# Splitting each half of a paired matmul step into a step of its own, with new places for score and maximum units, in a windowed-attention layer

## The chip, the cores and the metric

The kernel runs on one core of one Trainium2 chip. The metric is the device time of one execution in microseconds, the median of several runs. TensorE (PE in the profile; its weight loads are PEld), VectorE (DVE), ScalarE (ACT) and GpSimd (POOL) each work through their own instructions in order; SyncE (SP) issues all transfers. They meet at semaphores only.

## The reference

A post-norm transformer layer over 16 rows (batch entries) of 512 tokens and 256 features, 16 heads of 16 features, windows of 128 tokens:

```python
qkv = (x @ Wqkv + bqkv).reshape(B, S, 3, H, Dh)
scores = jnp.einsum('bhnqd,bhnkd->bhnqk', qb, kwin) * scale     # each window sees itself and both neighbours
mask = (jnp.abs(kpos - qpos) <= W) & (kpos >= 0) & (kpos < S)
attn = jax.nn.softmax(jnp.where(mask, scores, -1e30), axis=-1)
out = jnp.einsum('bhnqk,bhnkd->bhnqd', attn, vwin) @ Wout + bout
x = layernorm(x + out)
h = relu(x @ Wq1.T + b1)                                        # Wq1, Wq2: weights rounded to -1, 0, 1
x = layernorm(x + h @ Wq2.T + b2)                               # 256 -> 1024 -> 256
```

## The kernel before

**One row, many stages.** The outer loop (`steps`, positions `at` = -2 to 16) handles a row per position, and several rows at once: while the attention of row `b` runs, the row before it goes through output projection, norms and feed-forward (the steps named in `POST`), and the row after it through its query, key and value projections. A position has four parts (`v` = 0 to 3), one for each quad of heads. I call one position a *turn* of the loop; most of them do the same work.

**Side steps.** `SIDE[v]` lists the steps of a part in TensorE's order: `qk` (query and key projection, two of them), `vp` (values), `nmt` (transposes the negative row maxima), `pv` (probabilities times values, 32 matmuls), `ut` and `ot` (transposes back), `op` (output projection), `ln1`, `x1` and `x1t` (norm, its result, its transpose), four `f1` and two `f2` (feed-forward), `xs`, `xr` and `ln2`. Most of TensorE's side steps write a pair of PSUM banks out of `shared` (two pairs, `N_PAIRS = 2`), and a step that takes a pair waits until its last reader is done (`pair_free`, line 479).

**Two halves.** The contraction is cut into the lower and upper 64 partitions. `in_halves` (line 522) and `transposes_in_halves` (line 544) issue matmuls in couples, one on each half of the array, into different banks. Once every matmul of the first half of the step is issued, the banks are exchanged, and TensorE waits on its own semaphore `s_half` until the first half has drained. Both halves are in one step. `passed()` between couples lets score and maximum units in.

**Score and maximum units.** A part has 12 score units S0 to S11 (`scores`, line 500: keys times queries into `st`, read by ScalarE's exponential, line 749) and 12 maximum units M0 to M11 (`max_scores`, line 516, into `mx`, read by VectorE, line 899) for a quad two parts on. Each has two banks, so unit i waits until the reader of unit i-2 is done. S and M work on opposite halves of the array. `weave` puts them in six groups S, M, S, M, preferably where halves are exchanged (`RUN = 2`).

**Order elsewhere.** VectorE follows `dve_order` with a `LAG` for each kind of step, ScalarE follows the list itself, with its share of a step before or after the step's exponentials, POOL masks the probabilities when units 5 and 11 are through (line 1059), and SP follows `TRANSFERS`.

## Time and profile before

| | before |
|---|---|
| runs | 1175.44 us median of 3 (1175.4 to 1178.41) |
| profiled execution | 1178.41 us, span 1176.7 us, mean granted TensorE clock 0.904 |
| instructions | 28808, of them PE matmuls 10628 |

An instruction's duration in the timeline contains the filling and draining of the array; matmuls on the two halves of the array and successive ones overlap, so the distance between starts says what one costs. PEclk is the granted TensorE clock as a share of 2.4 GHz: 1.00 is 2.4 GHz, 0.50 is 1.2 GHz, and a value between is a mix of the two over the stretch. An idle time in front of a group is put down to the engine whose semaphore came last.

### The profile page before, as it was taken

What the parts mean: (1) busy time and instruction counts of PE and PEld (TensorE: products, weight loads), DVE (VectorE), ACT (ScalarE), POOL (GpSimd) and SP (SyncE); (2) the same over time, 40 slices, a digit from 0 to 9 for tenths busy, and PEclk for the clock granted to TensorE, in tenths of its full rate; (3) what the DMA queues carried; (4) which work ended last, traced back from release to release, by engine and by line L of the source; (5) the groups of instructions that cost most, each with busy time, mean ns of one, the idle gap of its engine ahead of it and who ended that gap; (6) DMA issues with size and microseconds to landing.
All of it is one profiled execution on the core that took longest, in us unless ns stands there. A gap on an engine that the chain in (4) does not pass through costs nothing.

```text
span 1176.7 us, 28808 instructions
## 1 busy us (share of the span) xinstructions
PE 973.5 (83%) x10628; PEld 772.5 (66%) x10628; DVE 813.6 (69%) x2900; ACT 704.1 (60%) x1401; POOL 612.6 (52%) x951
## 2 busy tenths in 40 slices
PE   4798887988798888979798898879888797977866
PEld 2474776766676676767577676767677676666644
DVE  3785868678685867768686767768686867866222
ACT  3254765849485665848476584848567584835613
POOL 1124464655656555655655466565645465554522
PEclk8587899989999898999899899989989998997967
DMA  8654334344452543454263434445254434431000
GB/s 194 71 87 74 48 64 81 60 80 74 75 91 38 93 64 73 66 92 74 58 92 55 81 61 79 75 79 86 39 95 63 81 57 74 74 61 33 11 9 18
DMA packets 58026, 81.82 MB, mean 70 GB/s; under 512 B 8736, under 2 KB 28704, under 8 KB 57888
## 3 DMA queue, kind: packets, MB, share of 16 engines
q1 hardware_dynamic: 57888, 79.99, 40.9%
q8 instruction: 85, 1.39, 0.6%
q14 instruction: 53, 0.43, 0.2%
HBM read 20.19 MB, written 8.39 MB: 24 GB/s over the span
## 4 chain that ended last, share of the span: by engine, by line
PE 47%; ACT 22%; DVE 14%; issue 9%; POOL 4%; DMA 2%; SPq 1%; DVEq 0%; ACTq 0%; POOLq 0%
PE shared L538 24%; PE st L500 8%; PE shared L586 7%; DVE mx L899 7%; ACT probs L749 6%; ACT hidden L825 5%; PE mx L516 5%; ACT hid_hi L828 4%; ACT x L807 2%; PE shared L558 2%; ACT oT_x1T_hi L813 1%; DVE rmax L899 1%; ACT qk_hi L773 1%; POOL probs L1059 1%; PE shared L599 1%
## 5 line engine op out<-in xcount | busy, mean ns | idle before, releaser
L899 DVE CUSTOM_DVE_ANT_0 mx<-mx,band 128x384 f32<-128x384 f32 (+1 forms) x1024 | 479.0, 517 | 250.4 <-PE mx L516 245.5
L749 ACT ACTIVATE probs<-st 128x384 f32<-128x384 f32 (+1 forms) x768 | 365.3, 524 | 186.8 <-PE st L500 183.6
L516 PE MATMUL mx<-k_stack,q_stack 48*128 48x384 f32 (+1 forms) x1024 | 290.7, 371 | 22.3 <-DVE rmax L899 17.2
L1059 POOL TENSOR_SCALAR_AFFINE_SELECT probs<-probs 128x512 f32<-128x512 f32 (+1 forms) x256 | 127.8, 524 | 311.0 <-ACT probs L749 311.0
L500 PE MATMUL st<-q_stack,k_stack 50*128 50x384 f32 (+1 forms) x1024 | 266.7, 355 | 12.3 <-ACT probs L749 7.0
L500 PEld LDWEIGHTS st<-q_stack,k_stack 50*128 50x128 f32 x1024 | 183.8, 209 | 63.7 <-issue 30.7
L516 PEld LDWEIGHTS mx<-k_stack,q_stack 48*128 48x128 f32 x1024 | 186.0, 210 | 50.0 <-DVE rmax L899 39.5
L586 PE MATMUL shared<-probs,v_aug 128*32 128x384 f32 (+1 forms) x2048 | 165.1, 448 | 9.4 <-POOL probs L1063 7.2
L538 PE MATMUL shared<-w2q,hid_hi 64*128 64x256 f32 x1024 | 158.3, 306 | 2.0 <-POOL hid_lo L1104 1.7
L538 PE MATMUL shared<-w2q,hid_lo 64*128 64x256 f32 x1024 | 150.2, 295 | 0.0
L899 DVE DVE_READ_ACCUMULATOR2_ANT rmax<- 128x1 f32 x1024 | 144.2, 141 | 0.0
L538 PEld LDWEIGHTS shared<-w2q,hid_hi 64*128 64x128 f32 x1024 | 132.2, 203 | 3.6 <-ACT hid_hi L828 1.9
L538 PEld LDWEIGHTS shared<-w2q,hid_lo 64*128 64x128 f32 x1024 | 133.7, 203 | 0.0
L1104 POOL TENSOR_TENSOR hid_lo<-hidden,hid_hi 128x512 fp32r<-128x512 f32 x64 | 82.5, 1289 | 88.8 <-ACT hid_hi L828 88.8
L586 PEld LDWEIGHTS shared<-probs,v_aug 128*32 128x32 f32 x2048 | 91.2, 112 | 56.0 <-issue 19.3
L1063 POOL TENSOR_SCALAR_AFFINE_SELECT probs<-probs 128x512 f32<-128x512 f32 (+1 forms) x256 | 127.7, 524 | 0.0
L538 PE MATMUL shared<-oT_x1T_hi,w1q 64*128 64x512 f32 x512 | 115.6, 419 | 6.3 <-ACT hidden L825 2.0
L538 PE MATMUL shared<-oT_x1T_lo,w1q 64*128 64x512 f32 x512 | 111.7, 406 | 0.0
L825 ACT ACTIVATE hidden<-shared,b_cols 128x512 f32<-128x512 f32 x128 | 87.1, 680 | 15.1 <-PE shared L538 14.0
L792 ACT ACTIVATE u<-shared 128x512 f32<-128x512 f32 x64 | 37.5, 585 | 84.0 <-PE shared L586 84.0
L828 ACT ACTIVATE hid_hi<-hidden 128x512 fp32r<-128x512 f32 x128 | 80.8, 631 | 4.1
L982 DVE TENSOR_TENSOR hid_lo<-hidden,hid_hi 128x512 fp32r<-128x512 f32 x64 | 51.9, 810 | 40.2 <-ACT hid_hi L828 39.5
(99 smaller groups left out, 1883.5 us busy)
## 6 DMA issues: line engine op xcount, KB each, us to landing
q_stack<-qk_hi SPq DMA_DIRECT2D x128, 128.0 KB, 4.2
k_stack<-qk_hi SPq DMA_DIRECT2D x128, 128.0 KB, 5.0
x_raw<-in_xT SPq DMA_DIRECT2D x16, 512.0 KB, 5.8
q_stack<-qk_lo SPq DMA_DIRECT2D x64, 128.0 KB, 3.9
k_stack<-qk_lo SPq DMA_DIRECT2D x64, 128.0 KB, 5.5
y<-in_x SPq DMA_DIRECT2D x16, 512.0 KB, 6.3
out<-x SPq DMA_DIRECT2D x32, 256.0 KB, 2.2
probs<-in_w2T SPq DMA_DIRECT2D x1, 1024.0 KB, 10.2
```

The lines of the kernel that those rows point to most:

```text
L500: mm = pe.matmul(PST[i % N_SCORE][:, col:col + n], SK[rows, hd, W * m:W * m + W], SQ[rows, hd, q0:q0 + n], start=True, stop=True)
L516: mm = pe.matmul(PMX[i % N_MAX][:, col:col + n], SQ[rows, hd, W * m:W * m + W], SK[rows, hd, k0:k0 + n], start=True, stop=True)
L538: mm = pe.matmul(out[k][:, cols], lhs(rows), rhs(rows), start=(swap == 0 and n == 0), stop=(swap == 1 and n == count - 1), skip_group_chec ...
L586: mm = pe.matmul(out[0][32 * g:32 * g + 32, q0:q0 + width], VAUG[:, vq, m, g, :], PR[:, vq % 2, g // 2, lo:lo + width], start=(m == 0), st ...
L749: act.activation(PR[:, v % 2, g // 2, lo:lo + n], PST[i % N_SCORE][:, 0:n], ACT.Exp, scale=SCALE) \
L825: act.activation(H32[:, i, :], PG[:, 2 * k + i, :], ACT.Relu, bias=B1C[:, f:f + 1]) \
L828: act.activation(HID[0][:, f, :], H32[:, i, :], ACT.Identity).then_inc(s_hh, 1)
L899: mx = dve.tensor_tensor_reduce(ps, ps, band, 1.0, -3e38, ALU.add, ALU.max, RMAX[:, g, m:m + 1])
L982: dve.tensor_tensor(HID[1][:, f, :], H32[:, i, :], HID[0][:, f, :].bitcast(F32), ALU.subtract).then_inc(s_hld, 1)
L1059: pool.affine_select(out=pr_before, in_=pr_before, compare_op=ALU.is_ge, fill=0.0, base=0, pattern=[[0, n], [1, W]], channel_multiplier=-1)
L1063: last = pool.affine_select(out=pr_after, in_=pr_after, compare_op=ALU.is_ge, fill=0.0, base=0, pattern=[[0, n], [-1, W]], channel_multipl ...
L1104: pool.tensor_tensor(HID[1][:, f, :], H32[:, i, :], HID[0][:, f, :].bitcast(F32), ALU.subtract).then_inc(s_hlp, 1)
```

## The change

1. Each halved step becomes two entries of `SIDE`: `("start", ...)` issues the first half, the plain name the second, with the wait for `s_half` at its front. Other steps may stand between: `start qk 0`, `nmt`, `pv`, `ut 0`, `qk 0`; `start vp`, `start op`, `vp`, `op`. `pairs` hands out the two bank pairs as a queue through the whole loop.
2. `ut` is no longer tied to the `pv` of its part: the third part has none, the fourth has two. The `f1` steps follow one another; `vp` moves from between them to the first part. `ln2` comes at the end of the fourth part.
3. The 12 score and 12 maximum units of a part have places of their own, two tables in thousandths of the part's cost (`SCORES_AT`, `MAXIMA_AT`), so S and M units no longer come in couples.
4. Dummy matmuls (`WARM`): 12 couples a turn of 512 columns each on constant weights, in front of six steps, 384 matmuls in all.
5. ScalarE gets an order of its own (`act_order`, `ACT_LAG`), VectorE's lags go by single step, `TRANSFERS` is reordered, the loop has one more position (empty), and `scores` no longer waits for another quad's stack.
6. `REST_ON_POOL` shrinks from four `hid_lo` subtractions a turn on POOL (0, 2, 4, 6) to one (3), the others go to VectorE; one of four `x1` normalisations moves from ScalarE to VectorE.

```diff
 SIDE = [
-    ["nmt", "pv", "ut", "ot", "op", ("ln1", 0), ("ln1", 1), ("ln1", 2), ("ln1", 3)],
-    [("qk", 0), ("x1", 0), ("x1", 1), "nmt", "pv", ("x1", 2), "ut", ("x1", 3), "x1t", ("qk", 1), ("f1", 0)],
-    [("f1", 1), "vp", ("f1", 2), ("f1", 3), "nmt", "pv", "ut", ("xs", 0), ("xs", 1)],
-    [("f2", 0), ("ln2", 0), "xr", ("ln2", 1), "nmt", "pv", "ut", ("f2", 1), ("ln2", 2), ("ln2", 3)],
+    [("start", "qk", 0), "nmt", "pv", ("ut", 0), ("qk", 0), ("start", "ot"), "ot", ("start", "vp"),
+     ("start", "op"), "vp", "op", ("ln1", 0), ("ln1", 1), ("ln1", 2)],
+    [("ln1", 3), ("x1", 0), ("start", "qk", 1), ("qk", 1), ("x1", 1), ("x1", 2), "nmt", "pv", ("x1", 3),
+     ("ut", 1), ("start", "x1t"), "x1t", ("start", "f1", 0), ("f1", 0), ("start", "f1", 1), ("f1", 1),
+     ("start", "f1", 2)],
+    [("f1", 2), ("start", "f1", 3), "xr", ("f1", 3), "nmt", "pv", ("start", "f2", 0), ("f2", 0)],
+    [("start", "f2", 1), ("ut", 2), ("xs", 0), ("f2", 1), ("xs", 1), "nmt", "pv", ("ut", 3), ("ln2", 0),
+     ("ln2", 1), ("ln2", 2), ("ln2", 3)],
 ]
-REST_ON_POOL = (0, 2, 4, 6)
-X1_ON_DVE = ()
-RUN = 2
+REST_ON_POOL = (3,)
+X1_ON_DVE = (0,)
+SCORES_AT = ((57, 63, 184, 334, 424, 487, 492, 504, 606, 632, 712, 872),
...
+MAXIMA_AT = ((121, 126, 221, 289, 550, 575, 633, 708, 807, 844, 970, 995),
...
+WARM = {("ut", 0): 3, ("start", "x1t"): 1, ("ut", 1): 1, ("start", "qk", 1): 2, ("start", "f1", 3): 2,
+        ("start", "f1", 0): 3}
...
                     pe.wait_ge(s_nmin[v], 16 * b + 16)
-                    pe.wait_ge(s_nmin[v], 16 * b + 16)
-                    if v < 2 or stages(at)[2]:
-                        pe.wait_ge(s_stk[(v + 2) % 4], 96 * (b + v // 2) + 96)
...
-            def in_halves(out, terms, filled, passed, ready=None):
+            def one_half(out, terms, filled, passed, second, ready=None):
                 count = len(terms[0])
+                if second:
+                    exchange(passed)
+                for n in range(count):
+                    if n > 0 or not second:
                         passed()
...
+                    for rows, k in ((LOWER, second), (UPPER, 1 - second)):
...
+                for _ in range(WARM.get(whole_step, 0) if fresh else 0):
+                    for i, rows in enumerate((LOWER, UPPER)):
+                        pe.matmul(out[i], WQKV[0][rows, 0, 0:P], WQKV[0][rows, 1, 0:S], start=True, stop=True)
```

**Place 1: TensorE from the first part's `ut` to `op`.** Before: L599 is `ut`, L558 on `o_norm` is `ot`, L538 on `wout` is `op`, `st` and `mx` are score and maximum units.

```order
L500 MATMUL st<-q_stack,k_stack 128x384
L516 MATMUL mx<-k_stack,q_stack 128x384
L500 MATMUL st<-q_stack,k_stack 128x384
L516 MATMUL mx<-k_stack,q_stack 128x384
L599 MATMUL shared<-identity,u 128x64 x8
L558 MATMUL shared<-identity,o_norm 128x64 x8
L500 MATMUL st<-q_stack,k_stack 128x256 x2
L516 MATMUL mx<-k_stack,q_stack 128x256 x2
L500 MATMUL st<-q_stack,k_stack 128x384
L516 MATMUL mx<-k_stack,q_stack 128x384
L558 MATMUL shared<-identity,o_norm 128x64 x8
L538 MATMUL shared<-wout_hi,oT_x1T_hi 128x256 x2
```

And in the changed kernel: L671 are dummies, L697 is `ut 0`, L630 on `wqkv` is the second half of `qk 0`, L648 is `ot`, L589 are scores.

```order
L671 MATMUL shared<-wqkv_hi 128x512 x6
L697 MATMUL shared<-identity,u 128x64 x8
L589 MATMUL st<-q_stack,k_stack 128x384
L630 MATMUL shared<-xT_hi,wqkv_hi 128x512 x2
L630 MATMUL shared<-xT_hi,wqkv_lo 128x512 x2
L630 MATMUL shared<-xT_lo,wqkv_hi 128x512 x2
L589 MATMUL st<-q_stack,k_stack 128x384
L630 MATMUL shared<-xT_hi,wqkv_hi 128x512 x2
L630 MATMUL shared<-xT_hi,wqkv_lo 128x512 x2
L630 MATMUL shared<-xT_lo,wqkv_hi 128x512 x2
L648 MATMUL shared<-identity,o_norm 128x64 x6
L589 MATMUL st<-q_stack,k_stack 128x256 x2
```

The second half of `qk 0` has come between `ut` and `ot`, and the maximum units are gone from there; behind `ot` now comes `vp`, not `op`.

**Place 2: TensorE from the second part's `ut` to what follows `x1t`.** Before (L558 on `x` is `x1t`, L538 on `xT` is `qk 1`):

```order
L599 MATMUL shared<-identity,u 128x64 x8
L558 MATMUL shared<-identity,x 128x64 x8
L500 MATMUL st<-q_stack,k_stack 128x384
L516 MATMUL mx<-k_stack,q_stack 128x384
L500 MATMUL st<-q_stack,k_stack 128x256 x2
L516 MATMUL mx<-k_stack,q_stack 128x256 x2
L558 MATMUL shared<-identity,x 128x64 x8
L538 MATMUL shared<-xT_hi,wqkv_hi 128x512 x2
L538 MATMUL shared<-xT_hi,wqkv_lo 128x512 x2
L538 MATMUL shared<-xT_lo,wqkv_hi 128x512 x2
```

In the changed kernel (L605 is a maximum unit, L630 on `w1q` is `f1 0`):

```order
L671 MATMUL shared<-wqkv_hi 128x512 x2
L697 MATMUL shared<-identity,u 128x64 x8
L671 MATMUL shared<-wqkv_hi 128x512 x2
L648 MATMUL shared<-identity,x 128x64 x8
L589 MATMUL st<-q_stack,k_stack 128x384
L648 MATMUL shared<-identity,x 128x64 x8
L671 MATMUL shared<-wqkv_hi 128x512 x6
L630 MATMUL shared<-oT_x1T_hi,w1q 128x512 x2
L605 MATMUL mx<-k_stack,q_stack 128x384
L630 MATMUL shared<-oT_x1T_lo,w1q 128x512 x2
```

`qk 1` no longer stands between `x1t` and `f1 0`; three dummy couples and one score unit do.

**Place 3: TensorE at the second part's first score units.** Before, in the middle of `qk 0`:

```order
L538 MATMUL shared<-xT_lo,wqkv_hi 128x512 x2
L500 MATMUL st<-q_stack,k_stack 128x384
L516 MATMUL mx<-k_stack,q_stack 128x384
L500 MATMUL st<-q_stack,k_stack 128x384
L516 MATMUL mx<-k_stack,q_stack 128x384
L538 MATMUL shared<-xT_hi,wqkv_hi 128x512 x2
L538 MATMUL shared<-xT_hi,wqkv_lo 128x512 x2
```

In the changed kernel, at the start of `qk 1`, right behind the last matmuls of `op`:

```order
L630 MATMUL shared<-wout_lo,oT_x1T_hi 128x256 x2
L671 MATMUL shared<-wqkv_hi 128x512 x4
L589 MATMUL st<-q_stack,k_stack 128x384 x2
L589 MATMUL st<-q_stack,k_stack 128x256 x2
L630 MATMUL shared<-xT_hi,wqkv_hi 128x512 x2
L589 MATMUL st<-q_stack,k_stack 128x384 x2
L630 MATMUL shared<-xT_hi,wqkv_lo 128x512 x2
L589 MATMUL st<-q_stack,k_stack 128x256 x2
L630 MATMUL shared<-xT_lo,wqkv_hi 128x512 x2
L589 MATMUL st<-q_stack,k_stack 128x384
L630 MATMUL shared<-xT_hi,wqkv_hi 128x512 x2
```

Seven score units, which stood in four groups with maximum units before, now follow one another with three couples of `qk 1` between them.

## Rows read from the trace of the kernel before

**Rows 1.** The page: busy time by engine, and the chain that ended last.

```profile
PE 973.5 (83%) x10628; PEld 772.5 (66%) x10628; DVE 813.6 (69%) x2900; ACT 704.1 (60%) x1401; POOL 612.6 (52%) x951
...
PE 47%; ACT 22%; DVE 14%; issue 9%; POOL 4%; DMA 2%; SPq 1%; DVEq 0%; ACTq 0%; POOLq 0%
```

**Rows 2.** Chain in order of time: start, us, what; `x1t`'s evacuation, seven turns apart.

```profile
202.09 1.09 ACT oT_x1T_hi L813 x2
...
672.54 1.09 ACT oT_x1T_hi L813 x2
```

**Rows 3.** Stretches: us, PE, PEld, DVE, ACT, POOL busy (instructions), PEclk, DMA share, GB/s.

```profile
279.04:344.97 65.93, 56.16 (x668) 44.89 (x666) 49.65 (x181) 43.39 (x88) 38.45 (x60) 0.97 0.44 74
```

**Rows 4.** Waits of PE over the span: total us, times, longest.

```profile
PE shared L599 <- ACT u L792: 31.7, 46, 1.4
PE shared L538 <- DVE oT_x1T_lo L945: 27.5, 16, 1.8
PE shared L558 <- DVE o_norm L940: 19.2, 16, 1.4
PE shared L558 <- ACT x L807: 18.2, 32, 4.6
PE mx L516 <- DVE rmax L899: 17.2, 39, 0.8
PE shared L576 <- DVE neg_max L910: 16.6, 16, 1.9
...
PE shared L586 <- POOL probs L1063: 7.2, 14, 0.5
```

**Rows 5.** Stretches as in rows 3: `vp`, `f2 1`, `op`.

```profile
278.82:283.90 5.08, 4.87 (x65) 4.11 (x61) 4.70 (x13) 4.80 (x11) 2.19 (x2) 1.00 1.08 117
303.30:309.75 6.45, 5.68 (x80) 5.16 (x78) 5.49 (x26) 2.83 (x6) 5.38 (x9) 1.00 0.73 109
319.39:326.05 6.66, 6.66 (x73) 6.49 (x75) 5.11 (x20) 4.13 (x10) 1.95 (x4) 0.74 1.03 151
```

**Rows 6.** Timeline of PE: couples at two clocks, and a score unit beside a side step.

```profile
321.12 0.45 PE L538 MATMUL shared<-wout_hi,oT_x1T_lo 64*128 64x256 f32 x2
321.34 0.45 PE L538 MATMUL shared<-wout_lo,oT_x1T_hi 64*128 64x256 f32 x2
...
322.94 0.30 PE L538 MATMUL shared<-wout_hi,oT_x1T_lo 64*128 64x256 f32 x2
323.06 0.30 PE L538 MATMUL shared<-wout_lo,oT_x1T_hi 64*128 64x256 f32 x2
...
324.82 0.33 PE L500 MATMUL st<-q_stack,k_stack 50*128 50x384 f32 x1
324.88 0.28 PE L538 MATMUL shared<-wout_hi,oT_x1T_lo 64*128 64x256 f32 x1
...
328.00 0.43 PE L538 MATMUL shared<-xT_hi,wqkv_lo 64*128 64x512 f32 x2
328.23 0.43 PE L538 MATMUL shared<-xT_lo,wqkv_hi 64*128 64x512 f32 x2
```

**Rows 7.** Stretches as in rows 3, around the first part's `ut`, `ot` and `op`.

```profile
314.60:317.90 3.30, 1.64 (x30) 1.42 (x30) 2.32 (x10) 1.05 (x4) 2.76 (x6) 1.00 0.26 93
317.90:321.20 3.30, 1.81 (x16) 1.84 (x18) 2.66 (x9) 2.59 (x6) 0.00 (x0) 0.73 1.00 153
```

**Rows 8.** Groups by form: line engine operation, busy us, mean ns; of evacuations and units' readers.

```profile
L749 ACT ACTIVATE probs<-st 128x384 f32<-128x384 f32 x512 | 238.3, 489 | 115.7 <-PE st L500 112.5
...
L825 ACT ACTIVATE hidden<-shared,b_cols 128x512 f32<-128x512 f32 x128 | 87.1, 680 | 15.1 <-PE shared L538 14.0 <-POOL hid_lo L1104 0.2
...
L1104 POOL TENSOR_TENSOR hid_lo<-hidden,hid_hi 128x512 fp32r<-128x512 f32 x64 | 82.5, 1289 | 88.8 <-ACT hid_hi L828 88.8
...
L982 DVE TENSOR_TENSOR hid_lo<-hidden,hid_hi 128x512 fp32r<-128x512 f32 x64 | 51.9, 810 | 40.2 <-ACT hid_hi L828 39.5
...
L976 DVE TENSOR_TENSOR oT_x1T_lo<-shared,oT_x1T_hi 128x512 fp32r<-128x512 f32 x32 | 20.5, 682 | 5.3 <-ACT oT_x1T_hi L813 5.2
```

## The prediction made before the changed kernel ran

> **What bounds the kernel now.** I read the page's first and fourth part first. TensorE is the busiest engine and the last chain runs through it for 47%, with ACT at 22% and DVE at 14% [rows 1]: no engine is full, and a few engines take turns. The chain in order of time repeats itself: the same evacuation comes at 202.09 and, seven turns later, at 672.54 [rows 2], so a turn takes 470.45 / 7 = 67.2 us, and what is saved in a turn is paid back about 15 times (the positions 1 to 15; the first three and the last do part of the work). In one turn of 65.9 us TensorE is busy 56.2 us, DVE 49.7, ACT 43.4, POOL 38.5 [rows 3]. So the reader is to look for two things: the 9.7 us in which TensorE stands, and the part of its busy time in which it isn't issuing at its rate.
>
> The waits say where it stands [rows 4]. Over the span: on the evacuation of `u` 31.7 us, on `oT_x1T_lo` before `op` 27.5, on `o_norm` before `ot` 19.2, on `x1` before `x1t` 18.2 (4.6 of it once, at the end), on a maximum's reader 17.2, on the negative maxima 16.6, on the mask 7.2. Most of these are short and come once a turn: a step whose input the step just before it made.
>
> **What TensorE's own work costs.** Couples of 256 columns start 0.12 us apart (322.94, 323.06) and of 512 columns 0.23 us apart [rows 6]. A unit of 384 columns on one half is then 0.17 us, one of two blocks of 256 0.24, on average 0.19, and an S and an M in couple, on opposite halves, cost 0.19 together. With this, stretches can be compared with their content [rows 5]. `vp`: 24 couples and 4 couples of units are 2.9 + 0.8 = 3.7 us, it took 5.08. `f2 1`: 32 x 0.12 + 6 x 0.19 = 5.0, it took 6.45. `op`: 24 x 0.12 + 8 x 0.19 = 4.4, it took 6.66 at PEclk 0.74, that is 52% of it at 1.2 GHz, which costs 1.7, and leaves 0.5. So 1.4 + 1.5 + 0.5 = 3.4 us are lost there because units come in groups with both readers to be waited for; that is 18 of the turn's couples of units, and I take 5.5 us for the whole turn.
>
> **The change, part by part, for one turn.**
>
> *Gaps at `ot` and `op`.* The wait on `o_norm` is 1.2 us (19.2 / 16) and that on `oT_x1T_lo` 1.7 (27.5 / 16) [rows 4]. Half of `qk 0` (six couples of 512 columns, 1.4 us, and two score units) now lies in front of `ot`, and `start vp` in front of `op`. That covers both: -2.9. Late next is `start vp`, whose bank pair is that of `qk 0`: its two `hi` and two `lo` evacuations take some 2.3 us from the end of `qk 0` (0.6 and about 0.7 each, nearest row L976 at 0.68 [rows 8]), and `ot` with its three score units is only 1.5: +0.8. Term: -2.1.
>
> *The transposes of `u`.* Before, two couples of units stood between `pv` and `ut`, and TensorE still waited up to 1.4 us [rows 4]. Now up to five maximum units in a run stand there, with two banks: they go at the reader's pace, and such a run lasts about 2.3 us where the old slot lasted 2.1; in the third part no `ut` follows at all. The slots hold 12 lone maximum units more and cost about the same. Term 0 (-1.5 to +1.5).
>
> *Other waits.* `nmt` no longer follows the last maximum directly: 16.6 / 16, -1.0. The mask: `pv` of the first part comes after `start qk 0`: -0.4. `x1t` has `qk 1`, `pv` and a run of units in front of it, and its chain (`y`, four statistics, POOL, four `x1`) is about as long as they are: -0.5 of 0.9. Term: -1.9 (-2.5 to 0).
>
> *Places of units.* S and M no longer need their readers at the same moment. Of the 5.5 us I take half back, because runs of scores are a new grouping. Term: -2.7 (-5.5 to +1).
>
> *Clock.* After a stretch in which TensorE was busy 1.64 of 3.30 us, at `ut` and `ot`, the granted clock fell to 0.73 [rows 7], with couples of `op` 0.21 instead of 0.12 us apart [rows 6]. The 1.7 us lost there should mostly go when `qk 0` fills the place. Term: -1.4 (-1.7 to 0). The Trainium skill (TensorE: Matmul & The Clock Gate, the section on the clock gate) says that the slow clock is the default state and that activity releases it; by that the dummies help only where a fall is near, and this trace agrees that within most of a turn the clock is at 1.00.
>
> *S and M apart.* Counting the order, 16 of 48 couples remain neighbours and 12 M stand in the slots behind `pv`. Outside those slots I count some 49 lone units and 12 couples, where there were 40 couples: 61 x 0.19 = 11.6 against 7.6 us. A lone unit can overlap with the other half: at 324.82 a score unit and at 324.88 a matmul of `op` run together [rows 6]. Term: +2.5 (+0.5 to +4.0). The same page of the Trainium skill (the section on packing small matmuls) has a rule that speaks against the change: matmuls are strictly in order at start and end, none is let past. Rows 6 agree as far as the starts go. By it a lone unit that waits for its reader holds back the couples behind it on both halves, and this term would be its upper end.
>
> *Dummies.* 12 couples x 0.23 = 2.8 us of issue. Those before `ut` and `x1t` fall into waits in part, those before `start qk 1`, `start f1 0` and `start f1 3` in part: +1.0 (0 to +2.8). In the last turn, with no units, they are hidden by the waits.
>
> *New waits.* `f1 0` follows `x1t` directly. Its first matmul needs ACT's `hi` and DVE's `lo` (0.6 and 0.68 [rows 8], with the handing over 1.5 us); three dummy couples and a score unit cover 0.8: +0.7. The four `f1` in a row ask ACT for 8 times two passes, the first 0.68 us [rows 8] and the second about as long, some 10 us, while TensorE has 32 x 0.23 = 7.5 and some ten units: +0.8, and `pv` of the third part waits for a mask whose exponential is behind `f1 1` on ACT. Seven scores in a row at 0.49 an exponential [rows 8] need 3 us where 2.5 us of work is: +0.5. Behind these scores on PE stands `qk 1`, and behind that everything. With overlap between the three: +2.0 (+0.5 to +4).
>
> *Moves between engines.* Three subtractions of 0.81 us and one `x1` add 2.9 us to DVE's 49.7 a turn and take 3 x 1.29 from POOL [rows 3, 8]. DVE at 52.6 of 64 is still covered, but its queue gets tighter; that is in the range. The removed waits on other stacks were met long before: 0. In the last turn `hid_lo` at 0.81 instead of 1.29 in the chain: -1 in all. SP's new order puts transfers later than before but all a part ahead of their use: 0. The empty loop position costs nothing.
>
> **The sum.** -2.1 + 0 - 1.9 - 2.7 - 1.4 + 2.5 + 1.0 + 2.0 = -2.6 us a turn, x 15 = -39, and -1 at the end: -40. The profiled execution took 1178.41 us (1.7 above its span), 3.0 above the median of 1175.44. 1178.4 - 40 = 1138, on the median's scale 1135; I say 1136. The ends of the eight terms together, as independent errors, are about 4.5 us a turn; most of the time the error is within 3.2, or 48 us.
>
> **The rivals.**
>
> *A. The units starve TensorE (slower).* In the second part seven scores, then five maxima stand in runs, each unit held to its reader, and DVE has 2.9 us more a turn. If the runs cost 1 us each at five places instead of nothing, and the `f1` row 2 us more because ACT and DVE are both behind, the sum turns from -2.6 to about +1.2, with a part of it already in the terms: 1176 + 18 = 1194. It decides when more than 2.6 of these 7 us come true. For it: waits on maximum readers are already 17.2 us [rows 4] with runs of only two. Against: DVE and ACT have 16 and 22 us free in a turn [rows 3].
>
> *B. TensorE becomes full (faster).* If nearly all waits go and lone units overlap, a turn is its content, some 50 us at full clock, with dummies and what is left of drains 62: -5.2 a turn, 1098. For it: the order puts another step between almost every producer and its user. Against: content alone already grows by S and M apart.
>
> *C. The change moves waits, not the turn (no change).* What ACT and DVE have to deliver between two dependent steps is the same, and TensorE waits later for the same: 1175.
>
> **Chances.** Forecast 0.60, A 0.18, B 0.15, C 0.07. A difference of 0.3%, 3.5 us, is about what a measurement of this kernel can tell. Faster by more than that: forecast and B, 0.75. Same: C, 0.07. Slower: 0.18. Range 1090 to 1184: the forecast's 48 us, reaching most of B and a part of A.
>
> **What would show it.** In the profile after: no wait of `op` on `oT_x1T_lo` and of `ot` on `o_norm`; a new one before `start vp` on `qk_lo` and one before `f1 0` on `oT_x1T_lo`; mean clock above 0.93; TensorE's busy time about 960 to 1000 us with 384 matmuls more; a turn of 64.6 us. If the waits go and the turn stays, it is C, or A if waits of `st` on `probs` and of `mx` on `rmax` have grown to 50 us and more. The forecast is wrong most easily in the two terms on the units, -2.7 and +2.5, which rest on counting, not on a row.

## The result, and the profile after

The changed kernel takes 1278.9 us (median of 4 runs, 1276.0 to 1281.4), the kernel before 1175.4 us (4 runs on the same chip). The ratio is 1.0885, 95% interval [1.0839, 1.0931]: about 9% slower. The forecast was 1136 us, faster, so it failed in direction and by 143 us. The profiled run took 1278.94 us (span 1277.2, mean granted clock 0.911; before 0.904).

The page of the changed kernel, busy time by engine and the chain that ended last, against [rows 1]:

```profile
PE 1098.1 (86%) x11012; PEld 841.3 (66%) x11012; DVE 847.9 (66%) x2964; ACT 715.2 (56%) x1385; POOL 565.4 (44%) x903
...
PE 66%; ACT 13%; DVE 11%; POOL 5%; issue 3%; DMA 1%; SPq 0%; POOLq 0%; DVEq 0%; ACTq 0%
```

One turn as in [rows 3]: length, busy time of PE, PEld, DVE, ACT and POOL (instructions), PEclk, DMA share, GB/s:

```profile
598.72:671.99 73.27, 65.41 (x690) 50.79 (x690) 51.53 (x184) 44.07 (x87) 35.46 (x56) 0.94 0.41 68
```

And the waits of PE over the span, as in [rows 4], with one line of the kernel before that [rows 4] does not show (L500):

```profile
PE mx L605 <- DVE rmax L996: 68.3, 108, 4.9
PE st L589 <- ACT probs L848: 33.6, 63, 1.5
PE shared L684 <- POOL probs L1160: 15.2, 15, 1.5
PE shared L671 <- DVE qk_lo L1023: 11.5, 15, 0.8
...
PE shared L630 <- DVE oT_x1T_lo L1073: 2.5, 16, 0.2
...
PE st L500 <- ACT probs L749: 7.0, 6, 2.5
```

A turn is 73.3 us instead of 67.1. The waits of [rows 4] on `o_norm`, on `neg_max` and on the evacuation before `op` have gone as forecast, and that on `u` with them, for which the forecast had nothing. In their place TensorE waits 68 us for readers of maxima (17 before), 34 for exponentials (7 before), and 11.5 for `qk_lo` in front of the dummies. TensorE's idle time is even smaller than before (179 us against 203), yet its busy time grew by 125 us. The dummies are 192 couples x 0.23 = 44 us of that. For the rest I have only a reading: a matmul counts as busy over its whole stay, and short waits between lone units disappear in that.

**Where in the turn.** From the timeline of PE I took, in every turn, the start of the first `ot` matmul as zero, and from there the end of `op`, the first `nmt` behind it, the start of the last `pv` matmul, the first matmul of `x1t` and of `f1 0`, and the next `ot`. Means over 13 turns, us:

```
kernel                          op end   nmt    pv     x1t    f1 0   turn
before                          10.02    13.10  15.28   16.96  23.56  67.09
changed                         11.17    17.65  19.83   25.73  28.75  73.27
e8  new order, old rules        11.08    14.62  16.80   23.13  26.63  73.58
e9  scores spread               11.18    15.09  17.27   25.93  28.95  73.10
e10 lo and norms first          11.17    17.32  19.50   23.44  26.38  71.20
e14 e10, maxima ahead of pv     11.17    19.54  21.82   23.52  26.67  71.15
e4  before, S and M apart       11.08    14.49  16.67   18.66  26.76  71.40
e1  old order, new engines      10.05    13.15  15.33   17.12  23.51  66.83
e6  e1 and ten dummy couples     8.74    11.89  14.07   15.80  22.51  64.94
e7  e1 and half of qk 0 moved   11.90    14.27  16.45   18.97  25.66  72.16
e12 e6 and half of qk 0 moved   11.81    14.32  16.50   19.04  25.86  72.00
e17 e12, units kept             10.73    13.10  15.28   17.77  24.13  67.31
```

Up to `op` the changed kernel does `vp` as well (24 couples), and behind `x1t` it doesn't do `qk 1`; from `ot` to `f1 0` both kernels do the same amount of side work. It takes 28.75 us against 23.56, so 5.2 of the 6.2 us lost in a turn lie there, and between the end of `op` and `x1t`, with one `qk`, one `nmt` and one `pv` in both, 14.6 us against 6.9. Two things must be counted against this comparison. The changed kernel also issues seven dummy couples (1.6 us) between `ot` and `f1 0`, and its score and maximum units lie elsewhere: 42 of their matmuls in that stretch where there were 54, and 19 where there were 10 between `op` and `x1t`. Behind `f1 0` it has 12 more of them and takes only 1.0 us longer. And the turns are not the whole loss: the first `ot` of all comes 14.7 us later than before (131.4 against 116.7).

**What happens there.** The timeline of the changed kernel, from the score units that follow `op` (place 3) to `f1 0`: start, length, engine, line, operation; in brackets the idle time before it and what ended it. L1050 makes `y`, L1062 the norm statistics, L1068 and L906 `x1`, L872 is `qk_hi` of `qk 1`, L605 a maximum unit, L996 reads a maximum unit, L697 is `ut 1`:

```profile
655.67 0.38 PE L589 MATMUL st<-q_stack,k_stack 50*128 50x256 f32 x1 [0.65 <-ACT probs L848]
...
656.05 1.28 DVE L1050 TENSOR_TENSOR y<-shared,y 128x512 f32<-128x512 f32 x2
...
656.86 0.44 PE L589 MATMUL st<-q_stack,k_stack 50*128 50x384 f32 x1 [0.27 <-ACT probs L848]
...
658.47 0.93 PE L630 MATMUL shared<-xT_hi,wqkv_lo 64*128 64x512 f32 x2
...
660.05 0.57 DVE L996 CUSTOM_DVE_ANT_0 mx<-mx,band 128x384 f32<-128x384 f32 x1 [1.33 <-PE mx L605]
...
660.87 0.30 DVE L1062 BATCH_NORM_AGGREGATE ln_mv<-ln_stats 128x2 f32<-128x6 f32 x2
...
662.29 1.27 ACT L872 ACTIVATE qk_hi<-shared,bqk 128x512 fp32r<-128x512 f32 x2 [3.21 <-PE shared L630]
...
664.65 0.44 PE L605 MATMUL mx<-k_stack,q_stack 48*128 48x384 f32 x1
...
665.38 0.57 DVE L996 CUSTOM_DVE_ANT_0 mx<-mx,band 128x384 f32<-128x384 f32 x1 [4.21 <-PE mx L605]
...
665.86 0.41 DVE L1068 TENSOR_SCALAR x<-y,ln_mv,ln_rstd 128x256 f32<-128x256 f32 x1
666.14 0.61 ACT L906 ACTIVATE x<-y,ln_neg_mean_rstd,ln_rstd 128x256 f32<-128x256 f32 x1
...
667.42 1.41 DVE L1023 SCALAR_TENSOR_TENSOR qk_lo<-shared,bqk,qk_hi 128x512 fp32r<-128x512 f32 x2
...
668.88 0.79 PE L671 MATMUL shared<-wqkv_hi 64*128 64x512 f32 x2 [0.76 <-DVE qk_lo L1023]
...
669.48 0.63 PE L697 MATMUL shared<-identity,u 64*128 64x64 f32 x8
...
670.44 0.63 PE L648 MATMUL shared<-identity,x 64*128 64x64 f32 x8
```

VectorE stands still for 4.21 us, though `qk_hi` of `qk 1` is done at 663.56 and its `x1` is due. It stands because the next item in its fixed order is a maximum whose unit TensorE issues only behind `pv`, at 664.65. Behind that item stand one `x1`, three more maxima and `qk_lo`, behind `qk_lo` (its bank pair is the next to be used) the dummies and `ut 1`, and behind these `x1t`. The last `x1` is done at 666.75, so what `x1t` waits for longest is `qk_lo` and not the norm. (The turn shown is one of the three slowest; in most turns VectorE stands for 3.6 us.) The same stretch of the kernel before, for comparison:

```profile
327.20 1.27 DVE L953 TENSOR_TENSOR y<-shared,y 128x512 f32<-128x512 f32 x2
...
330.10 0.30 DVE L965 BATCH_NORM_AGGREGATE ln_mv<-ln_stats 128x2 f32<-128x6 f32 x2
330.34 0.57 DVE L899 CUSTOM_DVE_ANT_0 mx<-mx,band 128x384 f32<-128x384 f32 x1
...
331.34 1.40 DVE L926 SCALAR_TENSOR_TENSOR qk_lo<-shared,bqk,qk_hi 128x512 fp32r<-128x512 f32 x2
...
333.17 0.31 PE L558 MATMUL shared<-identity,x 64*128 64x64 f32 x4
```

Here the maxima on which VectorE could wait were issued ahead of `pv`, all statistics end before them, and from `y` to `x1t` it is 6.0 us; in the changed kernel it is 14.4, and 13.1 in the mean of 13 turns.

### The profile page after: what moved, and what is told of

It reads as the page before. It is cut to its first block, busy times and chain, and to the rows that moved or that the text cites. A ratio compares the mean times of both kernels' runs of the same rounds, so it can differ in the third digit from the quotient of the medians.

```text
span 1277.2 us, 29491 instructions
## 1 busy us (share of the span) xinstructions
PE 1098.1 (86%) x11012; PEld 841.3 (66%) x11012; DVE 847.9 (66%) x2964; ACT 715.2 (56%) x1385; POOL 565.4 (44%) x903
## 4 chain that ended last, share of the span: by engine, by line
PE 66%; ACT 13%; DVE 11%; POOL 5%; issue 3%; DMA 1%; SPq 0%; POOLq 0%; DVEq 0%; ACTq 0%
PE shared L630 29%; PE shared L684 12%; PE st L589 11%; DVE mx L996 6%; PE mx L605 6%; ACT hidden L924 4%; ACT hid_hi L927 3%; PE shared L671 3%; ACT probs L848 3%; DVE qk_lo L1023 2%; PE shared L648 2%; POOL probs L1160 2%; ACT oT_x1T_hi L899 2%; POOL probs L1156 2%; POOL hid_lo L1201 2%
## 5 line engine op out<-in xcount | busy, mean ns | idle before, releaser
L996 DVE CUSTOM_DVE_ANT_0 mx<-mx,band 128x384 f32<-128x384 f32 (+1 forms) x1024 | 483.4, 515 | 267.3 <-PE mx L605 262.1
L848 ACT ACTIVATE probs<-st 128x384 f32<-128x384 f32 (+1 forms) x768 | 378.8, 526 | 289.6 <-PE st L589 282.2
L605 PE MATMUL mx<-k_stack,q_stack 48*128 48x384 f32 (+1 forms) x1024 | 312.3, 359 | 73.5 <-DVE rmax L996 68.3
L589 PE MATMUL st<-q_stack,k_stack 50*128 50x384 f32 (+1 forms) x1024 | 300.3, 352 | 34.2 <-ACT probs L848 33.6
L605 PEld LDWEIGHTS mx<-k_stack,q_stack 48*128 48x128 f32 x1024 | 184.4, 198 | 123.9 <-DVE rmax L996 117.4
L589 PEld LDWEIGHTS st<-q_stack,k_stack 50*128 50x128 f32 x1024 | 182.1, 197 | 93.1 <-ACT probs L848 59.2
L630 PE MATMUL shared<-w2q,hid_hi 64*128 64x256 f32 x1024 | 168.7, 289 | 2.5 <-ACT hidden L924 2.3
L630 PE MATMUL shared<-w2q,hid_lo 64*128 64x256 f32 x1024 | 169.9, 283 | 0.0
L996 DVE DVE_READ_ACCUMULATOR2_ANT rmax<- 128x1 f32 x1024 | 145.4, 142 | 0.0
L630 PE MATMUL shared<-oT_x1T_hi,w1q 64*128 64x512 f32 x512 | 137.1, 451 | 3.0 <-DVE oT_x1T_lo L1073 2.5
L630 PEld LDWEIGHTS shared<-w2q,hid_hi 64*128 64x128 f32 x1024 | 134.8, 187 | 5.6 <-ACT hidden L924 2.7
L630 PEld LDWEIGHTS shared<-w2q,hid_lo 64*128 64x128 f32 x1024 | 136.3, 187 | 0.0
L630 PE MATMUL shared<-oT_x1T_lo,w1q 64*128 64x512 f32 x512 | 125.4, 403 | 0.0
L671 PE MATMUL shared<-wqkv_hi 64*128 64x512 f32 x384 | 93.7, 515 | 14.7 <-DVE qk_lo L1023 11.5
L1079 DVE TENSOR_TENSOR hid_lo<-hidden,hid_hi 128x512 fp32r<-128x512 f32 x112 | 82.1, 744 | 34.0 <-ACT hid_hi L927 34.0
L630 PE MATMUL shared<-xT_hi,wqkv_hi 64*128 64x512 f32 x256 | 86.1, 485 | 12.7 <-DVE xT_lo L1017 11.3
L630 PEld LDWEIGHTS shared<-oT_x1T_hi,w1q 64*128 64x128 f32 x512 | 68.8, 193 | 36.8 <-PE shared L630 15.4
```

What stands on the lines that cost most here:

```text
L589: mm = pe.matmul(PST[i % N_SCORE][:, col:col + n], SK[rows, hd, W * m:W * m + W], SQ[rows, hd, q0:q0 + n], start=True, stop=True)
L605: mm = pe.matmul(PMX[i % N_MAX][:, col:col + n], SQ[rows, hd, W * m:W * m + W], SK[rows, hd, k0:k0 + n], start=True, stop=True)
L630: mm = pe.matmul(out[k][:, cols], lhs(rows), rhs(rows), start=n == 0 and not second, stop=n == count - 1 and bool(second), skip_group_chec ...
L671: pe.matmul(out[i], WQKV[0][rows, 0, 0:P], WQKV[0][rows, 1, 0:S], start=True, stop=True)
L848: act.activation(PR[:, v % 2, g // 2, lo:lo + n], PST[i % N_SCORE][:, 0:n], ACT.Exp, scale=SCALE) \
L996: mx = dve.tensor_tensor_reduce(ps, ps, band, 1.0, -3e38, ALU.add, ALU.max, RMAX[:, g, m:m + 1])
```

## The experiments

Ratios are to the kernel before, run on the same chip, with a 95% interval.

**First question: which part of the change costs?**

*e1, the moves between engines alone.* Old order of all five engines in the new code:

```diff
 REST_ON_POOL = (3,)
 X1_ON_DVE = (0,)
-SIDE, SCORES_AT, MAXIMA_AT, TRANSFERS, DVE_LAG, ACT_LAG: new
-WARM = {("ut", 0): 3, ...}
+SIDE, TRANSFERS, lags and groups of units as before
+WARM = {}
```

> The old order of all five engines word for word but for two things of the change: three of four hid_lo subtractions go from POOL to VectorE and one x1 from ScalarE to VectorE (and the waits on another quad's stack are gone); no dummies. The theory that the places of the units make the loss (P) expects 1165 to 1182. The rival that a fuller VectorE makes the maxima late (V: maxima wait 68 us in the changed kernel where they waited 17) expects over 1200.

Measured: 1171.1 us, 0.9961 [0.9930, 0.9992]. The engine moves and the dropped waits are worth 0.4% at most. The loss lies in the order.

*e2, the changed kernel without dummies.*

```diff
-WARM = {("ut", 0): 3, ("start", "x1t"): 1, ...}
+WARM = {}
```

> The changed kernel without its 384 dummy matmuls. Twelve couples of 0.23 us are 2.8 us a turn, 45 us in all if nothing hides them. P expects that most of them lie in waits for readers and only 10 to 25 us go: 1254 to 1269. The rival that the dummies are half the loss (D) expects 1228 to 1240, provided the clock does not fall; if they hold the clock up, the time stays at 1279 or rises.

Measured: 1300.2 us, 1.109 [1.103, 1.115]. On balance the dummies do not cost, they save 21 us; without them the mean granted clock is 0.865 instead of 0.911.

*e3, e5, e8: the changed order with units together.* In e3 the units come in groups S, M, S, M by a rule like the old one, in e5 both kinds stand at the mean of the two tables, in e8 the groups follow the old rule and the lags of VectorE and ScalarE are the old ones.

```diff
 e3, e8: weave() with RUN = 2, RUNS_AT = (0.95, 0.93)
 e8:     "pv": (2500, 1), DVE_LAG and ACT_LAG as before
 e5:     both = [(a + b) / 2 for a, b in zip(SCORES_AT[v], MAXIMA_AT[v])]
```

> The changed kernel, with its order of steps, dummies, engines and lags, but score and maximum units in six groups S, M, S, M a part again, one group where the two halves of a step meet directly. P expects the loss to go: 1150 to 1200. The rival that the new order of steps itself is slower (O: f1 in a row, values projection away from it) expects 1240 to 1290.

> The changed kernel with each score unit and its maximum unit at one place, the mean of their two places in the tables; everything else of the change stays (steps, lags, dummies). P (apart costs some 4 us a turn) expects 1200 to 1235. If what matters is only that readers are waited for (R: the waits of st on probs and of mx on rmax), coupling makes both be waited for at once: 1270 to 1340, as the version with groups showed 1337.

> The new order of side steps and the dummies, but units in groups S, M, S, M at the old rule's places and the old lags for VectorE and ScalarE. The order of steps is then alone with the dummies. O (the order itself is slower, with f1 in a row on ScalarE) expects 1230 to 1300; if the order is sound and only its tables are bad, 1150 to 1200.

Measured: e3 1336.6 us, 1.138 [1.130, 1.147], slower than either theory allowed; e5 1310.2, 1.114 [1.105, 1.122]; e8 1278.1, 1.0885 [1.0834, 1.0936]. With the old rules for units and lags, and the new side order and dummies, the time is that of the changed kernel. So the loss is there without the tables too, and the side order is enough for it (together with the new `TRANSFERS`, which stayed); the table above shows e8 better up to `x1t` and worse behind.

*e4, S and M apart in the kernel before*: maximum units one couple later than the score units.

```diff
-slot[k] += [(p, kind, u) for u in ... for kind in ("scores", "max")]
+slot[k] += [(p if kind == "scores" else p + 1, kind, u) for u in ... for kind in ("scores", "max")]
```

> The kernel before, where only the two maximum units of each group come one couple of matmuls later than its two score units, so they no longer share the array with them and where halves meet only two scores cover the drain. P expects 1200 to 1240: some 40 lone units a turn at 0.05 to 0.1 us, and up to 0.2 us at each of ten meetings of halves. If apart or together makes no difference by itself (O or V), 1170 to 1185.

Measured: 1243.8 us, 1.0595 [1.0545, 1.0645], 4.3 us a turn, just above the range. PE in e4, at the second of two lone score units:

```profile
345.24 0.34 PE L501 MATMUL st<-q_stack,k_stack 50*128 50x384 f32 x1
345.51 0.50 PE L539 MATMUL shared<-xT_hi,wqkv_hi 64*128 64x512 f32 x2
345.86 0.34 PE L517 MATMUL mx<-k_stack,q_stack 48*128 48x384 f32 x1
345.86 0.39 PE L539 MATMUL shared<-xT_hi,wqkv_lo 64*128 64x512 f32 x1
346.04 0.34 PE L517 MATMUL mx<-k_stack,q_stack 48*128 48x384 f32 x1
346.09 0.39 PE L539 MATMUL shared<-xT_lo,wqkv_hi 64*128 64x512 f32 x1
```

From 345.06 to the side matmul that starts at 346.21 it is 1.15 us. Five side matmuls lie in it, 2.5 x 0.23 = 0.58; so the four units cost 0.57, where the group in the kernel before took 0.44 (327.22 to 327.66) and wholly lone units would take 4 x 0.17 = 0.68. The table gives nearly the same: from `f1 0` to the next `ot`, where 11 groups are parted, e4 takes 1.1 us more, 0.10 a group, though the clock is at 1.2 GHz there no longer than before (1.8 us against 2.4). Over the 20 groups that e4 parts (the four behind `pv` stay together) that is an estimate of 2 to 2.6 of the 4.3 us. The rest goes with the clock: from `ot` to `f1 0`, where the other 3.2 us were lost on 9 groups, the clock is at 1.2 GHz for 11.0 us a turn instead of 5.5. In 12 of the 20 groups the maxima also no longer stand where the halves are exchanged; e4 doesn't tell these apart. TensorE's wait for maxima did not grow (12.9 us, 17.2 before), that for exponentials little (11.6, 7.0 before); its busy time grew by 68 us.

**Second question: can dummies help where they stand in a real wait?**

*e6, e18, e16: the old order with dummies.* e6 adds ten couples a turn to e1, e18 five; e16 adds ten to the kernel with the old split of engines as well.

```diff
+WARM = {("start", "ot"): 4, ("start", "op"): 6}     e6, e16
+WARM = {("start", "ot"): 2, ("start", "op"): 3}     e18
```

> The order of before with the three subtractions and one x1 moved to VectorE (1171 by itself), and ten dummy couples a turn in the two waits of the first part: four before ot, six before op. If the clock falls there for want of activity (C) and comes back to 2.4 GHz, the stretch of op runs at 0.12 us a couple and 1 to 1.7 us a turn go: 1146 to 1158. If the dummies only take time, they lengthen the waits by a little: 1172 to 1185.

> The old order with five dummy couples a turn (two before start ot, three before start op) instead of ten, which gave 1146.8 (0.977). If a part of a wait filled is enough to hold the clock, the time is the same, 1143 to 1152. If the wait must be filled through, about half of the gain: 1155 to 1165.

> The kernel before in every engine's order and split of work, with ten dummy couples a turn added: four before start ot, six before start op. With the engine moves they gave 1146.8 (0.977). Theory: the engine moves were worth 0.4% and the dummies the rest, so 0.977 to 0.985, 1148 to 1158 us.

Measured: e6 1146.8 us, 0.977 [0.9725, 0.9815]; e18 1144.5, 0.9755 [0.9708, 0.9802]; e16 1148.8, 0.9766 [0.9732, 0.9800]. These three beat both kernels and are the same to within their intervals. Two stretches of e6 around `ut`, `ot` and `op`, against [rows 7]:

```profile
635.10:638.40 3.30, 3.10 (x44) 2.55 (x46) 2.38 (x12) 1.11 (x3) 2.65 (x6) 1.00 0.28 97
638.40:641.70 3.30, 2.97 (x35) 2.25 (x31) 3.09 (x12) 2.80 (x7) 0.25 (x1) 1.00 0.99 156
```

PEclk is 1.00 where it was 0.73, and in the table `op` ends 1.3 us earlier than in e1. Over 13 turns the clock was at 1.2 GHz for 7.9 us a turn in the kernel before, 5.5 of them between `ot` and the end of `op`, and for 1.3 us in e6, none of them there. The dummies fit into the waits: those of `op` start 0.99 us behind the first `ot` matmul, and `op` starts no later (2.97 us behind `ot`, 3.04 without).

**Third question: why does the order cost?**

*e7, e12, e17: one move of the new order alone*, the first half of `qk 0` to between `ot` and `op`; e12 with the ten dummy couples; e17 as e12 with every score and maximum unit kept beside the side step it stood at in the old order.

```diff
-    ["nmt", "pv", ("ut", 0), ("start", "ot"), "ot", ("start", "op"), "op", ...
-    [("start", "qk", 0), ("qk", 0), ("x1", 0), ...
+    ["nmt", "pv", ("ut", 0), ("start", "ot"), "ot", ("start", "qk", 0), ("start", "op"), "op", ...
+    [("qk", 0), ("x1", 0), ...
 e12: +WARM = {("start", "ot"): 4, ("start", "op"): 6}
 e17: +WOVEN made from the old SIDE, then mapped to the new one
```

> The order of before (engine moves as above, no dummies), where only the first half of qk 0 moves from the second part to between ot and op, as real work in the wait on oT_x1T_lo; units stay in groups. The idea of the change by itself (I: halves as separate steps pay where they fill a wait) expects 1.7 us of wait and about 1 of clock a turn less: 1125 to 1150. If the wait only moves (later qk evacuation, units behind it), 1165 to 1180.

> The old order with one move (the first half of qk 0 between ot and op) and the ten dummy couples before ot and op that were worth 2.3% in the old order. Without dummies the move cost 80 us. Theory 'clock': the move was slow because start qk 0, qk 1 and x1t ran at 1.2 GHz; with the dummies it comes near the old order with dummies, 1150 to 1175. Theory 'cover': qk 0 was what covered the norm chain between op and x1t and the evacuation of oT at once, its units wait for an exponential behind that evacuation, and the move costs 3 us a turn at any clock: 1190 to 1220.

> The kernel e12 (old order, first half of qk 0 between ot and op, ten dummy couples) with the score and maximum units kept beside the side steps they stand at in the old order; in e12 the move had shifted the shares of cost, and so the places of all units of two parts: three groups had come into start qk 0, behind the evacuation of oT on ScalarE, and two groups close to each other at qk 1 and f1 0. Theory 'places': the 7 us a turn that e12 takes more than the old order with dummies come from those groups, and here the time is near it: 1145 to 1175. Theory 'cover': qk 0 is missing between op and x1t, whatever stands inside: 1190 to 1250.

Measured: e7 1251.4 us, 1.0659 [1.0613, 1.0705]; e12 1250.4, 1.0639 [1.0603, 1.0674]; e17 1187.9, 1.0108 [1.0057, 1.0158]. The move costs 80 us without dummies (e7 against e1) and 104 with them (e12 against e6); e7 and e12 missed both of their forecasts. At a mean clock of 0.924 (e12) the time is that at 0.883 (e7), so my theory that the cold clock makes the move dear fell: it isn't the main cause. e17 lies between its two: of the 104 us between e6 and e12, the places of the units are 63, and the other 41 remain when the units are kept. The places of units are shares of a part's cost, so moving one step moved all units of two parts. In e12 one group of units came at the end of `qk 1` and the next four couples later, while ScalarE and VectorE (L867, L1018) were evacuating `qk 1`:

```profile
575.55 1.26 ACT L867 ACTIVATE qk_hi<-shared,bqk 128x512 fp32r<-128x512 f32 x2 [0.95 <-PE shared L625]
...
576.28 1.41 DVE L1018 SCALAR_TENSOR_TENSOR qk_lo<-shared,bqk,qk_hi 128x512 fp32r<-128x512 f32 x2 [1.37 <-ACT qk_hi L867]
...
577.36 0.43 PE L584 MATMUL st<-q_stack,k_stack 50*128 50x384 f32 x1 [0.52 <-ACT probs L843]
...
578.52 0.43 PE L600 MATMUL mx<-k_stack,q_stack 48*128 48x384 f32 x1 [0.73 <-DVE rmax L991]
```

In e7 the units also hold up `op` itself. A group of them stands inside the moved half, behind an exponential that ScalarE does after `oT_x1T_hi`; VectorE's next item is a maximum of that group, and `oT_x1T_lo` stands behind it:

```profile
550.72 0.57 DVE L991 CUSTOM_DVE_ANT_0 mx<-mx,band 128x384 f32<-128x384 f32 x1 [1.35 <-PE mx L600]
...
551.20 1.41 DVE L1037 SCALAR_TENSOR_TENSOR oT_x1T_lo<-shared,bv_cols,oT_x1T_hi 128x512 fp32r<-128x512 f32 x2
```

In the mean `oT_x1T_lo` ends 5.88 us behind `ot` in e7 and 3.55 in e1, and `op` starts at 5.94 instead of 3.04. With the units kept (e17) `oT_x1T_lo` ends at 3.49, as in e6, and yet `op` starts at 5.04 instead of 2.97. PE in e17, from the end of the moved half to `op`:

```profile
660.63 0.40 PE L641 MATMUL shared<-xT_lo,wqkv_hi 64*128 64x512 f32 x2
661.93 1.66 PE L682 MATMUL shared<-wqkv_hi 64*128 64x512 f32 x12 [0.91 <-DVE oT_x1T_lo L1053]
663.43 0.28 PE L641 MATMUL shared<-wout_hi,oT_x1T_hi 64*128 64x256 f32 x2
```

The moved half takes one of the two bank pairs, so `op` gets the pair of `ot`, and its six dummy couples, which write that pair, wait for `oT_x1T_lo` too. They come behind the wait and not in it, and cost 1.5 us: some 24 of the 41 us (16 x 1.5, an estimate), and as much in e12. So the 41 us are not the price of the move alone; e17 without the dummies of `op` was not run. From the end of `op` to `x1t` e17 saves nothing against e6 (7.04 us, 7.06 there) though TensorE has a half step less to do.

*e9, e10, e11: the two suspects between `op` and `x1t` in the changed kernel.* e9 spreads the run of seven scores, e10 lets the norm steps and `qk_lo` pass the maxima on VectorE, e11 does both.

```diff
 e9:  -             (0, 0, 19, 24, 31, 56, 76, 278, 457, 582, 699, 949),
      +             (19, 76, 130, 185, 240, 300, 350, 400, 457, 582, 699, 949),
 e10: -DVE_LAG: ("ln1", 3): 1, ("x1", 0): 2, ("qk", 1): 3
      +DVE_LAG: ("ln1", 3): 0, ("x1", 0): 0, ("qk", 1): 0
```

> The changed kernel with one row of its table changed: the seven score units of the second part that stand in a run at the start of qk 1 are spread over the whole of qk 1 and the pv slot. From the end of op to the first matmul of nmt the changed kernel took 8.1 us where the same step with units in groups took 3.3 to 4.4. Theory 'the loss is local, at two places' says: that stretch falls to about 5 us, the turn by 2 to 3 us, 1235 to 1250 us in all. Rival 'the chain from ot to f1 0 sets the turn whatever lies in it': the 3 us come back as a wait before ut 1 or x1t and the time stays within 10 us of the changed kernel, 1268 to 1289.

> The changed kernel with three lags of VectorE set to 0 (ln1 3, x1 0, qk 1): the low part of qk 1 and the last norm statistics no longer stand behind three or four maxima whose units TensorE issues only after pv. In the changed kernel VectorE stood 4.2 us before these maxima and the next couple of TensorE waited for qk_lo. Theory 'local': the stretch from the end of pv to the first f1 0 falls from 8.8 us to 6.5 or 7, the turn by about 2 us, 1245 to 1260 us. Rival 'x1 is late anyway': u and x1t wait for x instead, 1270 to 1285.

> Both edits together. Theory 'local': they add up, about 4.5 us a turn, 1205 to 1225 us, which is still above the kernel before because f1 0 follows x1t directly and lone units stay. Rival 'one chain': no more than the better of the two alone.

Measured: e9 1279.6 us, 1.0884 [1.0846, 1.0922]; e10 1245.1, 1.0591 [1.0554, 1.0627]; e11 1259.0, 1.0711 [1.0678, 1.0744]. In e9 `nmt` comes 2.6 us earlier and `x1t` not at all: what the run of scores seemed to cost was slack in front of a later chain. The two edits don't add up either: e11 is slower than e10 alone, outside both of its forecasts. In e10 three numbers in VectorE's order take back 34 us, a third of the whole loss: `qk_lo` ends 4.8 us earlier and `x1t` comes 2.3 us earlier. The three were not changed one by one, so how much is `qk_lo` and how much the norm steps is not shown. VectorE in e10, where `qk_lo` follows `qk_hi` during `pv` and the maxima come after it:

```profile
574.35 1.41 DVE L1023 SCALAR_TENSOR_TENSOR qk_lo<-shared,bqk,qk_hi 128x512 fp32r<-128x512 f32 x2 [1.09 <-ACT qk_hi L872]
...
576.72 0.57 DVE L996 CUSTOM_DVE_ANT_0 mx<-mx,band 128x384 f32<-128x384 f32 x1 [0.96 <-PE mx L605]
...
577.40 0.44 PE L605 MATMUL mx<-k_stack,q_stack 48*128 48x384 f32 x1 [0.74 <-DVE rmax L996]
578.16 0.90 PE L605 MATMUL mx<-k_stack,q_stack 48*128 48x384 f32 x2 [0.33 <-DVE rmax L996]
```

*e13, e14, e15: what is left in e10.* e13 puts the last `hid_lo` on VectorE, e14 places maximum units of the second part inside `qk 1` instead of behind `pv`, e15 does both.

```diff
 e13: -REST_ON_POOL = (3,)
      +REST_ON_POOL = ()
 e14: -             (109, 276, 313, 353, 380, 388, 600, ...
      +             (109, 140, 175, 215, 245, 388, 600, ...
```

> The kernel e10 with its last hid_lo of a turn on VectorE instead of GpSimd (REST_ON_POOL empty). In e10's chain of waits ACT's passes over f1 run from 587.4 to 592.5, then hid_lo on POOL 1.29 us, then two masks 1.40 and 1.41, then pv: the masks stand behind hid_lo on POOL though their probabilities are older. Theory 'local': without it the masks start with the exponentials and pv of the third part comes 1.3 to 3 us earlier, 1200 to 1227 us. Rival 'ACT sets the f1 row': the mask's exponential is itself behind the passes of f1, and pv comes 0 to 0.5 us earlier: 1237 to 1250.

> The kernel e10 with four of the maximum units that follow pv in the second part placed inside qk 1. In e10's chain VectorE reads them one after the other from 576.7 to 578.6 between pv and ut 1. Theory 'local': x1t comes up to 2 us earlier and the turn falls by 1 to 2 us, 1215 to 1230. Rival 'norm chain': the norm statistics and x1 stand on VectorE in the same stretch and get later by what the maxima take, 1240 to 1265.

> Both edits on e10. If the losses of the new order are independent local ones, the sum of the two: 1180 to 1215 us. If one chain carries both, the better of the two.

Measured: e13 1248.8 us, 1.0607 [1.0566, 1.0649]; e14 1239.1, 1.0531 [1.0498, 1.0565]; e15 1240.2, 1.0544 [1.0510, 1.0578]. The masks do come earlier in e13, but the chain of waits then runs through ScalarE's passes of `f1` and VectorE's `hid_lo`; no time changes. Chain in e13, start, length, what:

```profile
592.85 0.58 ACT hidden L924
593.46 0.64 ACT hid_hi L927
594.12 2.88 DVE hid_lo L1079
597.00 0.34 DVE mx L996
```

In e14 the maxima are gone from behind `pv` and `nmt` is 2.2 us later for it; `x1t` comes at 23.52 instead of 23.44, and the turn is the same. The 6 us that are gained lie ahead of the turns: the first `ot` comes at 125.2 us instead of 131.8.

## Why the prediction was wrong

**The step that failed** is the one on `x1t` under "other waits": "`x1t` has `qk 1`, `pv` and a run of units in front of it, and its chain (`y`, four statistics, POOL, four `x1`) is about as long as they are: -0.5 of 0.9". I added the chain's durations as if VectorE ran them through, and left out `qk_lo`, which frees the bank pair that `ut 1` needs. In the changed order maxima stand between them whose units come only after `pv`; VectorE stands for 3.6 to 4.3 us, and the term that I had at -0.5 was a loss. e10 shows a part of it directly: 2.1 us a turn come back when the lags of `qk_lo` and two norm steps are set to 0. That is a third of the 6.2 us. Another 2.8 us between `ot` and `f1 0` are not taken apart: e9 and e14 show that units moved out of one place there come back as a wait at another. So of the 6.2 us a turn a third has a cause that a run shows, and two thirds have none.

**Places of units, -2.7.** Wrong in sign: waits on the readers of maxima and scores grew from 24 to 102 us. The 5.5 us of which I took half were also not worked out: 3.4 us for 18 of 48 couples of units would be 9 for the turn.

**S and M apart, +2.5.** e4 gives +4.3 us a turn in the old order, above the upper end of 4.0. By the estimate above only 2 to 2.6 of them are the parting itself, near my choice, and the rest is lost where the clock is low. That upper end was the one by the rule of the Trainium skill (TensorE: Matmul & The Clock Gate, the section on packing small matmuls), that none is let past another. e4 can't confirm the mechanism that I drew from the rule, a lone unit that waits for its reader and holds back the rest: in e4 the waits for maxima did not grow. In the changed order, though, the two effects don't simply add, since e8 with groups is as slow.

**New waits, +2.0.** The wait of `f1 0` was rightly seen and well covered (0.2 us a time instead of 0.7), and `x1t` to `f1 0` is 3.0 us. The run of seven scores costs nothing of its own (e9). What I didn't price is what a step's place does to VectorE's fixed order.

**Gaps at `ot` and `op`, -2.1.** Right in kind: the waits have gone and the one on `qk_lo` has come, but before the dummies of `ut 1`, not before `start vp`. With `vp` inside, `ot` to the end of `op` grew by 1.15 us, where `vp` alone had been 5.08 [rows 5]. But a gain there need not stay one: e7 and e17 show that a half step put in front of `op` also changes which bank pair `op` gets and, through the units inside it, when VectorE reaches `oT_x1T_lo`.

**Clock, -1.4, and dummies, +1.0.** The dummies were mis-sized in sign: -21 us (e2), that is -1.4 a turn. The mean clock is 0.911, not above 0.93. The fall in the first part has gone as forecast: from `ot` to the end of `op` the clock is at 1.2 GHz for 0.0 us a turn instead of 5.5. But from there to `f1 0` it is now 5.0 us where it was 0.0, and behind `f1 0` 3.2 instead of 2.4. In the turn shown, `ot` to `op` and then the stretch around `x1t`, as in [rows 3]:

```profile
643.36:654.50 11.14, 10.03 (x139) 9.26 (x137) 7.21 (x23) 7.01 (x13) 5.31 (x11) 1.00 0.59 97
667.00:676.00 9.00, 7.91 (x53) 6.08 (x55) 6.46 (x21) 1.79 (x4) 2.37 (x1) 0.62 0.92 138
```

Of the old order's own gaps, ten or five dummy couples take 2.3% (e6, e18), which the forecast never asked for, though [rows 7] had its price: 1.7 us a turn.

**The rivals.** It went nearest to A (waits on `probs` and `rmax` of 34 and 68 us, where I had named 50 and more), with a time 85 us above what I gave it. Its mechanism is part of the truth: units do starve TensorE, and a third of the loss comes through VectorE's order, in which a maximum that isn't issued yet holds back `qk_lo` and the norm. The moves between engines, at nearly nothing in the forecast, gave -0.4%.

**What stays open.** e14, the best of the changed order, is still 5% slower than the kernel before. The table puts 3.1 of its 4.1 us a turn between `ot` and `f1 0` and 0.9 behind. The move of `vp` and the row of four `f1` were not tried alone, nor was the new order of `TRANSFERS`, which e8 keeps; in the changed kernel, though, none of PE's waits in the list above or behind it in the profile is on a transfer. Why the first `ot` comes 14.7 us later was not looked into.

## What to carry to other kernels

When instructions are reordered on one engine, follow the fixed order of the engines that read its results: an item whose input is now issued later holds back all behind it, and the sum of durations says nothing about that. Where places are shares of a cost, moving one step moves everything else, so change one and pin the others before judging either. A step put into a wait takes its banks with it: look at which banks the next step then gets, and for whom it has to wait. And fill the waits that are there before reordering to remove them: five dummy couples a turn in the old order gave 2.4%, the reordering lost 9%.

## What the runs showed of the hardware

- In the kernel before, TensorE waits 1.2 us before `ot` and 1.7 before `op`, around steps of 64-column transposes, and the granted clock is then at 1.2 GHz for 5.5 of the 10.0 us from `ot` to the end of `op` (0.73 in [rows 7]). With two couples of 512 columns in one of these waits and three in the next the mean clock of the run was 0.949 (e18), with four and six 0.952 (e6), against 0.902 without (e1), and the times of e18 and e6 are the same.
- A score unit and a maximum unit of 384 columns on opposite halves of the array, issued in couples, cost 0.44 us for two of each; one couple of side work apart they cost 0.57 (one place in e4's timeline, and 0.10 us more a group over 11 groups a turn).
- Busy time is no measure of work here: at nearly the same mean clock (0.904 and 0.911) the changed kernel's PE is busy for 125 us more, of which its extra matmuls, the dummies, explain 44.
